# A fused cross-attention and quantised feed-forward kernel: the call order of all five engines laid anew, six groups of idle TensorE products left out

## The reference

```python
def xattn(x, ctx, mask):                       # x: layernorm of the input
    s = einsum('bsd,bmd->bsm', x, ctx) / sqrt(512)
    s = where(mask, s, -1e30)
    return einsum('bsm,bmd->bsd', softmax(s), ctx)

def bitlinear(x, w, b):
    x = x * rsqrt(mean(x * x) + 1e-5)
    q = 127 / clip(max|x|, 1e-5);  xq = clip(round(x * q), -128, 127) / q
    s = 1 / clip(mean|w|, 1e-5);   wq = clip(round(w * s), -1, 1) / s
    return xq @ wq.T + b

def ffn(x):                                    # 512 -> 2048 -> 512
    h = gelu(silu(bitlinear(x, w1, b1)))       # exact gelu
    return bitlinear(layer_norm(h, ln_g, ln_b), w2, b2)

x = x + xattn(layernorm(x), ctx, mask)
x = x + ffn(layernorm(x))
```

## Time and profile before

| | us |
|---|---|
| median of three runs | 419.5 (418.5 to 421.31) |
| the profiled execution, its own time | 421.23 |
| its span in the trace | 419.4 |
| around the span | 1.8 |
| ACT busy | 381.8 |
| PE busy (overlapping products counted whole) | 384.0 |
| DVE busy | 365.9 |
| POOL busy | 271.8 |

### The profile page before, as it was taken

How to read it: one execution, slowest core, us unless ns; L and a number is a source line. 1 busy time by engine, 2 the same in 40 slices (tenths; PEclk the granted TensorE clock), 3 DMA queues, 4 the chain that set the end, 5 groups by cost and what they waited for, 6 DMA issues and landing times.

```text
span 419.4 us, 6830 instructions
## 1 busy us (share of the span) xinstructions
PE 384.0 (92%) x1878; PEld 204.7 (49%) x1878; DVE 365.9 (87%) x571; ACT 381.8 (91%) x517; POOL 271.8 (65%) x373
## 2 busy tenths in 40 slices
PE   3899988789999999999999999999999987899996
PEld 2667353535545544544555454554455532344342
DVE  5278669989998989999999999989998789999992
ACT  1497999999999999999999999999999999999960
POOL 5358488764687838764785569585468855477930
PEclk9999998899999999999999999999999996999999
DMA  7998992556755677669668757694654423083484
GB/s 278 409 312 301 359 342 69 153 162 142 211 147 131 188 193 184 103 189 204 155 169 249 190 166 148 199 222 107 174 135 106 91 63 63 2 200 102 87 214 128
DMA packets 110389, 73.87 MB, mean 176 GB/s; under 512 B 87048, under 2 KB 87056, under 8 KB 109584
## 3 DMA queue, kind: packets, MB, share of 16 engines
q1 hardware_dynamic: 110352, 73.43, 65.1%
HBM read 44.05 MB, written 8.39 MB: 125 GB/s over the span
## 4 chain that ended last, share of the span: by engine, by line
issue 25%; ACT 21%; DVE 19%; PE 17%; POOL 13%; DMA 4%; SPq 1%; DVEq 0%; POOLq 0%; ACTq 0%
ACT junk_v L1212 6%; DVE hid L1981 5%; DVE hid L1972 5%; PE z L624 4%; PE acc L649 4%; ACT hid L1201 3%; ACT hid L1207 3%; POOL hid L1618 3%; PE ba L574 3%; ACT junk_l L1223 2%; POOL rstd L1607 2%; DVE am L1986 2%; POOL xc L1563 2%; DVE st L1900 1%; DMA hid<-in_w2T_dram 1%
## 5 line engine op out<-in xcount | busy, mean ns | idle before, releaser
L624 PE MATMUL z<-w1q,q1T 128*128 128x512 f16 x512 | 124.0, 386 | 3.3 <-ACT hid L1201 3.1
L649 PE MATMUL acc<-w2q,q2T 128*128 128x512 f16 x512 | 117.4, 379 | 0.4 <-DMA q2T<-hid 0.4
L1981 DVE SCALAR_TENSOR_TENSOR hid<-hid,rstd,beta 128x2048 f32<-128x2048 f32 x32 | 76.8, 2402 | 6.2 <-POOL rstd L1607 5.9
L624 PEld LDWEIGHTS z<-w1q,q1T 128*128 128x128 f16 x512 | 49.9, 99 | 65.6 <-ACT hid L1201 9.7
L1972 DVE SCALAR_TENSOR_TENSOR hid<-hid,nmu,gain 128x2048 f32<-128x2048 f32 x32 | 79.3, 2480 | 0.4 <-POOL nmu L1599 0.3
L649 PEld LDWEIGHTS acc<-w2q,q2T 128*128 128x128 f16 x512 | 49.8, 98 | 58.2 <-issue 0.9
L1986 DVE TENSOR_REDUCE am<-hid 128x1 f32<-128x2049 f32 x32 | 72.5, 2269 | 0.1
L1201 ACT ACTIVATE hid<-z,fac 128x1024 f32<-128x1024 f32 x64 | 70.7, 1119 | 1.6 <-PE z L629 1.4
L1223 ACT ACTIVATE junk_l<-hid 128x2050 bf16<-128x2050 f32 x32 | 61.1, 1910 | 4.1 <-DVE hid L1981 4.0
L1618 POOL TENSOR_SCALAR hid<-hid,kq 128x2048 f16<-128x2048 f32 x30 | 60.9, 2031 | 4.6 <-DVE kq L1993 3.1
L1212 ACT ACTIVATE junk_v<-hid,gsum 128x2048 bf16<-128x2048 f32 x32 | 63.7, 1990 | 0.1
(11 more groups left out here) (105 smaller groups left out, 572.2 us busy)
## 6 DMA issues: line engine op xcount, KB each, us to landing
ctxT<-in_ctxT_dram SPq DMA_DIRECT2D x32, 256.0 KB, 3.5
xs<-in_x_dram SPq DMA_DIRECT2D x32, 256.0 KB, 3.9
xT<-in_xT_dram SPq DMA_DIRECT2D x32, 256.0 KB, 3.6
ctx<-in_ctx_dram SPq DMA_DIRECT2D x32, 256.0 KB, 3.4
out_dram<-xs SPq DMA_DIRECT2D x32, 256.0 KB, 3.0
hid<-in_w1T_dram SPq DMA_DIRECT2D x4, 1024.0 KB, 10.2
hid<-in_w2T_dram SPq DMA_DIRECT2D x4, 1024.0 KB, 7.8
gain<-in_g_dram SPq DMA_DIRECT2D x1, 1024.0 KB, 11.1
```

What stands on the lines that cost most here:

```text
L624: pe.matmul(z_ps[h][:, c * CH:(c + 1) * CH], q1T[:, t % 4, k, :], w1q[:, k, f0:f0 + CH], start=(k == 0), stop=False)
L649: mm = pe.matmul(a, q2T[:, t % 2, c, :], w2q[:, c, :], start=False, stop=(c == FC - 1))
L1981: dve.scalar_tensor_tensor(out=hh, in0=hh, scalar=rstd[:, t:t + 1], in1=beta[:, :], op0=ALU.mult, op1=ALU.add).then_inc(s_l, 1)
```

## The change

The lists of calls of all five engines are laid anew. Every engine makes the same calls with the same arguments, onto the same tile buffers and semaphores, with these exceptions: PE's list loses `warm(9)` to `warm(14)`, that is 36 of the 120 idle products; of the plain waits in PE's list most are gone, which were repeated by the functions; and the loop in ACT's list is spelled out. The number of table loads on ACT is the same, 48. Line numbers fall by up to 117 for it.

At the head of SP's list (the first 21 calls of each):

```diff
-load_mask(0) load_ctxT(0) load_x(0) load_ctxT(1) load_xT(0) load_x(1) load_w1(0)
-load_mask(1) load_ctx(0) load_ctx(1) load_x(2) load_b2() load_ctxT(2) load_ctxT(3)
-load_b1() load_xT(1) load_x(3) load_w1(1) load_xT(2) load_w1(2) load_w1(3)
+load_ctxT(0) load_ctxT(1) load_xT(0) load_ctx(0) load_mask(0) load_b2() load_x(0)
+load_x(1) load_x(2) load_xT(1) load_x(3) load_ctxT(2) load_b1() load_ctxT(3)
+load_ctx(1) load_w1(0) load_w1(1) load_w1(2) load_xT(2) load_w1(3) load_xT(3)
```

PE's list at the idle products in the middle (`...` leaves calls out; the plain waits of before are not shown):

```diff
 scores(9)
-warm(9)
-turn_factors(4)
-turn_probs(8)
-first_product(4, 0)
-warm(10)
-column_sums(10)
+warm(6)
+readout(7)
+warm(7)
+column_sums(10)
+turn_factors(4)
+turn_factors(5)
+turn_probs(8)
+warm(8)
+first_product(4, 0)
...
 readout(31)
-warm(13)
 turn_factors(28)
-first_product(28, 0)
-warm(14)
 turn_factors(29)
+first_product(28, 0)
 first_product(28, 1)
```

ACT's list from the first weight sum to the first silu has these calls, before and after:

```diff
-mean_term(0) mean_term(1) weight_sum(0, 0) exp_scores(0) copy_probT(0) exp_scores(1)
-mean_term(2) copy_probT(1) mean_term(3) weight_sum(0, 1) weight_sum(0, 2) weight_sum(0, 3)
-exp_scores(2) square_x1(0) copy_probT(2) square_x1(1) exp_scores(3) copy_b1() round_w1(2)
-copy_probT(3) mean_term(4) square_x1(2) mean_term(5) exp_scores(4) square_x1(3)
-weight_sum(1, 0) exp_scores(5) copy_b2() silu(0, 0)
+mean_term(0) mean_term(1) exp_scores(0) copy_probT(0) exp_scores(1) copy_probT(1)
+weight_sum(0, 0) mean_term(2) mean_term(3) weight_sum(0, 1) square_x1(0) weight_sum(0, 2)
+square_x1(1) exp_scores(2) weight_sum(0, 3) copy_probT(2) round_w1(2) exp_scores(3)
+mean_term(4) mean_term(5) copy_b1() copy_probT(3) exp_scores(4) copy_b2() square_x1(2)
+copy_probT(4) weight_sum(1, 0) exp_scores(5) square_x1(3) silu(0, 0)
```

More of the change, by code:

```diff
@@ new lines, in _ @@
+            square_x1(14)
+            mean_term(18)
+            square_x1(15)
+            mean_term(19)
+            square_l(10)
+            copy_probT(17)
+            silu(13, 0)
+            silu(13, 1)
+            exp_scores(18)
+            exp_scores(19)
+            gelu(12)
+            square_x1(16)
+            square_x1(17)
+            copy_probT(18)
+            square_l(11)
+            gelu(13)
+            variance(12)
+            copy_probT(19)
+            variance(13)
@@ new lines, in _ @@
+            silu(14, 0)
+            silu(14, 1)
+            mean_term(20)
+            mean_term(21)
+            square_l(12)
+            silu(15, 0)
+            silu(15, 1)
+            gelu(14)
+            gelu(15)
+            variance(14)
+            exp_scores(20)
+            square_x1(18)
+            variance(15)
+            copy_probT(20)
+            exp_scores(21)
+            silu(16, 0)
+            silu(16, 1)
+            square_l(13)
+            mean_term(22)
+            mean_term(23)
@@ L1379, in _ @@
+            square_x1(19)
+            square_l(14)
+            copy_probT(21)
+            silu(17, 0)
+            square_x1(20)
+            silu(17, 1)
+            exp_scores(22)
+            exp_scores(23)
+            gelu(16)
+            gelu(17)
+            square_x1(21)
+            variance(16)
+            copy_probT(22)
             square_l(15)
-            variance(16)
-            gelu(17)
             copy_probT(23)
@@ L1461, in _ @@
             gelu(27)
-            square_x1(30)
             variance(26)
+            variance(27)
             square_x1(31)
-            variance(27)
             silu(28, 0)
+            silu(28, 1)
             square_l(24)
-            silu(28, 1)
             square_l(25)
```

1497 lines of the change are left out of this document (683 added, 814 removed).

## The result

The changed kernel takes 435.44 us (median of four runs, 433.37 to 436.69) against 419.56 for the kernel before beside it: 1.0366 times as long, 95% interval 1.0338 to 1.0394. By the medians that is 15.9 us. The forecast was 416.6 us, range 411 to 424. It was wrong, and on the wrong side.

A forecast was written before the change was run, and what follows sets the result against it. The prediction took ACT, working through its list end to end, as the bound. Start -0.3, middle -2.0 and tail -0.6 sum to -2.9: 418.3 us for the profiled execution, 416.6 us for the median, range 411 to 424.

The forecast's parts named there:

- The view and the bound: Whole kernel: ACT sets the time, 98.6% busy in the long middle; a new order wins only from its idle parts.
- The start: Up to ACT's first silu: w1 scale 1.0 us later, then 1.3 less idle; -0.3 us, between -3.3 and +3.
- The probabilities' path: In the start: without twelve idle products, tile 1's probabilities are ready 2 us or so earlier.
- The first rival: Start shorter than thought, giving -3.3, with middle -3.3 and tail -1; median 412.0 us, chance 0.33.
- The middle: From first silu to 402 us: 2.0 of 3.3 named us of ACT's waits won; -2.0 us, bounds -5.25 to +6.
- the upper end: Middle's bound of +6 us, if each of some 28 tiles gets a wait of 0.2 us more.
- the prediction's own sign against this step: More than 8 us of ACT idle time in the middle would prove the middle's step wrong.
- The clock and the idle products: In the middle, lost clock is fully hidden behind ACT, so leaving out the idle products there costs nothing.
- with ACT full beside it: Sign near 350 us: granted clock again about 0.5, while ACT stays full.
- The tail: Last second products: turn_factors(36) inside tile 29's product saves a gap; -0.6 us, bounds -1.5 to +1.
- The threshold of 15 us: A last second product starting more than 15 us after the last gelu would prove the tail's step wrong.
- the slower one: Second rival: PE's clock stays low in the start until about 38 us; median 425.0 us, chance 0.17.

The follow-up runs named there:

- b_dma: Kernel before with SyncE's first 22 loads in the changed kernel's order, nothing else; 424.33 us, ratio 1.0118.
- b_nowarm: Kernel before without the idle products warm(9) to warm(14), all other calls and waits in place; 419.54 us, ratio 0.9998.
- a_warm: Changed kernel with six groups of idle products put back on TensorE; 436.39 us, ratio 1.038.
- b_tail: Kernel before with the changed kernel's order at the very end on ScalarE, GpSimd and VectorE; 420.1 us, ratio 1.0016.
- ac_all: Changed kernel with early w2 clamps, earlier q1 transposes, factors-28 edit, variance(31) ahead of square_l(30), and two w1 clamps earlier; 426.64 us, ratio 1.0147.
- ac_stage: Changed kernel with early w2 clamps, and load_x(7), x_stats(7), x_rstd(6), mean_term(7) put back as in the kernel before; 428.41 us, ratio 1.0214.
- ac_all2: Changed kernel with early w2 clamps, plus ac_stage's edit, earlier q1 transposes, factors-28 edit and the old tail on three engines; 429.4 us, ratio 1.024.

## Why the prediction was wrong

**The view and the bound** were right: ACT sets the time; the longer span is its idle time (39.9 us up to its last instruction, 27.5 before, so 12.4) and 1.0 us of longer busy time.

**The start**, forecast at -0.3: the w1 scale was put at 28.3 and came at 26.91, the silu's table load at 39.0 and came at 38.26. The probabilities' path won more than its 2 us (tile 1's softmax at 14.23 instead of 17.41). The low clock came back from 11.3 to 18.2 us (granted 0.51) and cost what the forecast feared at the second column sums (3.27 us instead of 1.89), but nothing behind them: the third ones took 1.95 at 28.21. But the -1.0 of this pair of profiles isn't a gain: over all profiles the new start is 1 us later on average and scatters three times as far. The order of the loads was costed by the landing of x(0) and of the last piece of w1 alone; b_dma shows 5 us at stake in how each load stands to the call that needs it. The first rival, a shorter start, had no part in the result.

**The middle**, forecast at -2.0 within -5.25 to +6, measured +12.3: this is the step that failed, at the sentence "I see no cause for the upper end: DVE, which would have to be late, is itself idle for 29 us". That is an average over 363 us, and the cost came from single calls. Two clamps stood behind a reduction and a norm on DVE at the one moment when ACT had nothing else that it was allowed to do, and ACT waited 5.7 us. More than 8 us of idle time in the middle was the prediction's own sign against this step; it came to 17.55. The prediction argued with waits of 0.2 us for each tile; the loss is one wait of 5.7 and seven of 0.5 to 2.4. It also never asked which calls wait for w2. Silu's wait for all four pieces of it is no data of the silu; it guards the buffers, and it asks for the clamps too, which the buffers don't need. Going through the lists at each call that stands ahead of something ACT waits for, with the durations in the trace, would have shown it: reduction, norm and clamps are 2.3 + 2.4 + 1.4 us (the norm took 2.9 here).

**The clock and the idle products**, forecast as hidden: right in the kernel before (b_nowarm 0.9998), and putting them back into the changed kernel wins nothing. The place where cover is thin did come: behind 5.9 us of waiting the half product of tile 28 ran at half rate (3.43 us for eight products where 1.89 is the upper level's; the granted clock from 359.5 to 366.3 us was 0.50), and ACT waited 0.5 and 1.0 us for z. So the sign "with ACT full beside it" failed there. What made the cover thin was the order: a_warm has the idle products back and the same slow product.

**The tail**, forecast at -0.6, came out at about +1: the last second product starts 16.6 us after the last gelu ends, before 15.6. The threshold of 15 us that the prediction gave was therefore no test, since the kernel before failed it. The lists were called nearly the same, but those of VectorE and GpSimd differ too. The price of variance(31) behind square_l(30) was named but taken as half hidden; with the same order on GpSimd and VectorE it isn't (b_tail, 0.7 us in the time, 1.0 in ACT's idle time).

**The rivals**: the slower one, a low clock in the start, is not what happened, though its time of 425 was nearer; that nearness is chance. No rival had late calls of DVE.

**What is shown and what is open.** By cures, in the changed order, the clamps are 6 to 8 us. Three smaller places are 2.6 together, but under the old loads only; with the changed kernel's own loads they won nothing one by one, and 0.9 with two clamps of w1 (ac_all), inside the scatter. By mirrors, in the old order, clamps, factors, tail and loads are 10.7 of the 15.9. The mirror of the loads isn't a loss of the changed kernel itself, where they fit their list. So some 5 to 7 us of the 15.9 are not traced to a call: 1.0 is ACT's busy time, about 1 the later start on average; the rest is in waits of 0.3 to 1.2 us for z, w2 and the norm that moved when they were cured (ac_stage, ac_all2). Their cause stays open. No kernel tried beats the one before.

## What to carry to other kernels

In a kernel whose engines each follow a fixed list, ask of every moved call: which call of the bounding engine waits for it, including through a wait that guards a reused buffer, and what stands ahead of it in its own list, in microseconds from the trace. A mean idle share says nothing about it. Ask of the wait, too, whether it asks for more than the data and the buffer need. Orders are judged as sets: the loads and the five lists of one kernel fit each other, and a piece of another order, even a better one, can cost more than it brings.
